# Expert weight matrices fetched in two halves, each with a semaphore of its own

## The chip, the cores and the metric

The kernel runs on one core of a Trainium2 chip. The metric is the device time of one execution in microseconds (us), lower is better. Three runs of the kernel before took 686.67, 686.75 and 687.67 us, a median of 686.75 us.

## What is computed

One Perceiver layer in float32 over 8 batches of 64 tokens with 512 features: a cross attention with a context of 512 rows per batch, a linear attention, and a mixture of 16 experts beside a shared feed-forward network. The change lies in the experts alone. Cut to what matters:

```python
logits = jnp.einsum('bsd,ed->bse', hidden_states, gate_w)
scores = jax.nn.softmax(logits, axis=-1).transpose(0, 2, 1)
topk_w, topk_idx = jax.lax.top_k(scores, cap)              # cap = 8 tokens per batch and expert
x_tok = jnp.take_along_axis(hidden_states[:, None, :, :], topk_idx[..., None], axis=2)
g = jnp.einsum('becd,efd->becf', x_tok, Wg)                # Wg, Wu: 16 x (1024, 512)
u = jnp.einsum('becd,efd->becf', x_tok, Wu)
h = jax.nn.gelu(g, approximate=False) * u
eo = jnp.einsum('becf,edf->becd', h, Wd) * topk_w[..., None]   # Wd: 16 x (512, 1024)
...
shared = jnp.einsum('bsf,df->bsd', jax.nn.gelu(gs, approximate=False) * us, Ws_d)
return out + shared
```

Each expert has three matrices of 2 MB (512 x 1024 floats), so the experts read 48 matrices, 96 MB, from memory.

## The kernel before

The program is written by hand, one instruction stream per engine, tied by semaphores. The attentions come first, then the routing, then from about 421 us the list `ITEMS`: one eighth of the shared network first, then experts 0 and 1, an eighth, experts 2 and 3, an eighth, and so on, ending with expert 15 (`LAST`). A shared eighth is called `("s", i)` and an expert `("e", e)`.

**TensorE (PE).** For item n the order is `item_gate(n)`, `item_transpose(n - 1)`, `item_value(n)`, `item_down(n - 1)`. The first and third are `item_up` (products at L1409): for each of four slices `dt` of the 512 features, the tokens `x_slot` are loaded as weights of the array and `w_g` or `w_u` streams through it, 8 matmul instructions in the program, which the profile shows as 16 records. `item_down` (L1446) does the same with `w_d` and the transposed hidden values `hid_T`, with `j` over four slices. Each group waits once for its matrix, on `wg_in`, `wu_in` or `wd_in`. For the shared eighth the products are L1419 and L1459, with weights that are already on chip.

**The load queue.** The tiles `w_g`, `w_u` and `w_d` are doubled, so matrix e may be fetched when expert e - 2 has used its own. All loads are issued by SyncE (SP) in one fixed order, written out in the `for e in range(2, E, 2)` loop: for each pair of experts g(e), u(e), g(e+1), d(e), u(e+1), d(e+1). Each issue waits until the products of expert e - 2 are done. Transfers of one queue are served in the order of their issue. In memory each matrix lies with its partitions first, so that a partition's 16 KB are one contiguous run. In `w_g` and `w_u` these are the slices `dt` in order; in `w_d` they are the eight slices 0 to 7, of which product `j` reads slices j and 4 + j.

**Results.** The 64 result rows of an expert go by `send_row` (L380), eight transfers of 16 KB from chip memory to chip memory, into `eo_slot`. ScalarE (ACT) issues them for experts 0 to 12 on a queue of its own, SP issues all of expert 13 and the first half of expert 14, behind the last weight loads, and ACT the other half. TensorE sums them at the end (L1564), after a wait for all sends (`eo_sent`), then does `item_transpose(15)` and `item_down(15)`, and the last products (L1571) give the output.

```python
            item_gate(LAST)
            item_value(LAST)

            for par in range(2):
                pe.wait_ge(eo_sent[par], 16 * B * ((E - par) // 2))
```

Of the kernel before, what the change touches and what calls it, by code (L numbers as in the profile page):

```python
# [25 lines left out]
NT = TOK // P  # L26
KT = D // P
# [11 lines left out]
def perceiver_block(nc, x_d, ctx_d, wq_d, bq_d, wk_d, bk_d, wv_d, bv_d, wo_d, bo_d, wqkv_d, proj_d,  # L39
                    wout_d, bout_d, gate_d, wg_d, wu_d, wd_d, wsg_d, wsu_d, wsd_d, out_d):  # L40
    main = ExitStack()
    with main:
# [3 lines left out]
        def sem(name):  # L46
            return main.enter_context(nc.semaphore(name))
# [118 lines left out]
        w_u0 = sb(moe, "w_u0", [P, KT, FF])  # L166
        w_d0 = sb(moe, "w_d0", [P, NF, D])
# [3 lines left out]
        ws_d = sb(moe, "ws_d", [P, NF, D])  # L171
# [47 lines left out]
        w_g0 = sb(moe, "w_g0", [P, KT, FF])  # L219
# [37 lines left out]
        ctx0_in = [sem(f"ctx0_in{dt}") for dt in range(KT)]  # L257
        ctx_in, wqkv_in, wo_in, wout_in, rows_in = (sem(f"{n}_in") for n in ("ctx", "wqkv", "wo", "wout", "rows"))
        proj_in, gate_in = sem("proj_in"), sem("gate_in")
        wg_in, wu_in, wd_in = ([sem(f"{n}_in{i}") for i in range(2)] for n in ("wg", "wu", "wd"))  # L260
        ws_hi_done, ws_split, hid_hi_done, hid_split = sem("ws_hi_done"), sem("ws_split"), sem("hid_hi_done"), sem("hid_split")
        gate_hi_done, gate_split = sem("gate_hi_done"), sem("gate_split")
        wsg_in, wsu_in, wsd_in = sem("wsg_in"), sem("wsu_in"), sem("wsd_in")
# [110 lines left out]
        def g_stripe(i):  # L374

            return (i + 1) % NF

        def send_row(queue, e, b):
            row = SLOTS * (e % 2) + CAP * b
            queue.dma_start(eo_slot[CAP * e:CAP * (e + 1), b, :], eo_of(e)[row:row + CAP, :]).then_inc(eo_sent[e % 2], 16)  # L380
# [13 lines left out]
        @block.sync  # L394
        def _(sp):
            for dt in range(KT):
                sp.dma_start(wk_raw[:, dt], wk_d[:, dt]).then_inc(wk_in[dt], 16)
                sp.dma_start(ctx_raw[:, dt], ctx_d[0, :, dt]).then_inc(ctx0_in[dt], 16)
            for tile, src in ((bias_k, bk_d), (bias_q, bq_d), (bias_v, bv_d)):
                sp.dma_start(tile[:], src).then_inc(bias_in, 16)  # L400
            sp.dma_start(wv_raw[:], wv_d).then_inc(wv_in, 16)
            sp.dma_start(x[:], x_d.rearrange("(t p) d -> p t d", p=P)).then_inc(x_in, 16)
            sp.dma_start(wq_raw[:], wq_d).then_inc(wq_in, 16)
            sp.dma_start(bo_rows[:], bo_d.partition_broadcast(P)).then_inc(rows_in, 16)
            with sp.Fori(1, B) as b:
                sp.wait_ge(ctx_split, b + KT - 1)
                sp.dma_start(ctx_raw[:], ctx_d[b]).then_inc(ctx_in, 16)
            sp.dma_start(w_o[:], wo_d).then_inc(wo_in, 16)
            sp.dma_start(w_qkv[:], wqkv_d).then_inc(wqkv_in, 16)
            sp.wait_ge(x_done, NT)  # L410
            sp.dma_start(bout_rows[:], bout_d.partition_broadcast(P)).then_inc(rows_in, 16)
            for q in range(4):
                sp.dma_start(proj_twice[HD * q:HD * (q + 1)], proj_d[q % 2]).then_inc(proj_in, 16)
            sp.dma_start(w_out[:], wout_d).then_inc(wout_in, 16)
            sp.wait_ge(xbias_done, 2 * NT)
            sp.dma_start(gate[:], gate_d).then_inc(gate_in, 16)
            sp.wait_ge(qkv_lo_dve, KT)
            sp.wait_ge(qkv_lo_pool, 2 * KT)
            sp.dma_start(ws_g[:], wsg_d).then_inc(wsg_in, 16)
            sp.wait_ge(kv_ps, NT * KT)  # L420
            sp.dma_start(ws_u[:], wsu_d).then_inc(wsu_in, 16)
            sp.dma_start(w_u0[:], wu_d[0]).then_inc(wu_in[0], 16)
            sp.dma_start(w_d0[:], wd_d[0]).then_inc(wd_in[0], 16)
            sp.dma_start(ws_d[:], wsd_d).then_inc(wsd_in, 16)
            sp.wait_ge(att_done, 2 * NT)
            sp.dma_start(w_g0[:], wg_d[0]).then_inc(wg_in[0], 16)
            def expert_load(kind, e):

                tiles, src, arrived, used = {"g": (w_g, wg_d, wg_in, g_ps), "u": (w_u, wu_d, wu_in, u_ps),
                                             "d": (w_d, wd_d, wd_in, down_ps)}[kind]  # L430
                if e >= 2:
                    n = AT["e", e - 2]
                    sp.wait_ge(used, downs_upto(n) if kind == "d" else n + 1)
                sp.dma_start(tiles[e % 2][:], src[e]).then_inc(arrived[e % 2], 16)

            expert_load("g", 1)
            expert_load("u", 1)
            for e in range(2, E, 2):
                for kind, ahead in (("g", 0), ("u", 0), ("g", 1)):
                    expert_load(kind, e + ahead)  # L440
                if e == 2:
                    sp.wait_ge(give_ps, 2)
                    sp.wait_ge(last_T_done, NT)
                    expert_load("d", 1)
                for kind, ahead in (("d", 0), ("u", 1), ("d", 1)):
                    expert_load(kind, e + ahead)
            sp.wait_ge(g_ps, AT["s", NF - 2] + 1)
            for e in range(LATE, E - 1):
                sp.wait_ge(eo_done, e + 1)
                for b in range(B if e < E - 2 else B // 2):  # L450
                    send_row(sp, e, b)
            for t in range(NT):
                sp.wait_ge(y_done, t + 1)
                sp.dma_start(out_d[P * t:P * (t + 1), :], x[:, t, :]).then_inc(out_sent, 16)
            sp.wait_ge(out_sent, 16 * NT)
# [670 lines left out]
        def _(pe):  # L1126
# [203 lines left out]
            u = w = a = 0  # L1330
# [67 lines left out]
            def item_up(n, weights, shared_parts, off, in_, done):  # L1398


                dst = 2 * (n % 2) + off
                if n >= 2 and not is_expert(n - 2):
                    pe.wait_ge(sx_done, NT * shared_before(n - 2) + 2)
                if is_expert(n):
                    e = ITEMS[n][1]
                    pe.wait_ge(in_[e % 2], 16 * (e // 2 + 1))
                    for dt in range(KT):
                        for fh in range(2):
                            ins = pe.matmul(ps[64 * fh:64 * (fh + 1), dst, :], x_slot[:, e, dt, :],  # L1409
                                            weights[e % 2][:, dt, BANK * fh:BANK * (fh + 1)],  # L1410
                                            start=(dt == 0), stop=(dt == KT - 1), skip_group_check=True)
                else:
                    i = ITEMS[n][1]
                    hi, lo = shared_parts
                    pe.wait_ge(ws_split, 3 * i + off + 1)
                    for dt in range(KT):
                        w_hi_part, w_lo_part = hi[:, dt, :], lo(i)[:, dt, :]
                        for j, (a, c) in enumerate(((w_hi_part, xn_hi), (w_hi_part, xn_lo_moe), (w_lo_part, xn_hi))):
                            ins = pe.matmul(bank(dst), a, c[:, dt, :], start=(dt == 0 and j == 0),  # L1419
                                            stop=(dt == KT - 1 and j == 2))  # L1420
                ins.then_inc(done, 1)
# [16 lines left out]
            def item_down(n):  # L1438

                if is_expert(n):  # L1440
                    pe.wait_ge(hidT_done, experts_upto(n))
                    e = ITEMS[n][1]
                    pe.wait_ge(wd_in[e % 2], 16 * (e // 2 + 1))
                    for j in range(KT):
                        for fh in range(2):
                            ins = pe.matmul(ps[64 * fh:64 * (fh + 1), 6 + n % 2, :],  # L1446
                                            hid_T[:, n % 2, j, 64 * fh:64 * (fh + 1)], w_d[e % 2][:, KT * fh + j, :],
                                            start=(j == 0), stop=(j == KT - 1), skip_group_check=True)
                    ins.then_inc(down_ps, 1)
                else:  # L1450
                    i = ITEMS[n][1]
                    pe.wait_ge(ws_split, 3 * i + 3)
                    pe.wait_ge(hid_split, shared_before(n) + 1)
                    if shared_before(n):
                        pe.wait_ge(sx_done, NT * shared_before(n))
                    for t in range(NT):
                        rows = slice(P * t, P * (t + 1))
                        for j, (a, c) in enumerate(((hid_hi, ws_d_hi[:]), (hid_lo, ws_d_hi[:]), (hid_hi, ws_d_lo[:, i, :]))):
                            ins = pe.matmul(bank(shared_down_bank(n, t)), a[:, n % 2, rows], c, start=(j == 0), stop=(j == 2))  # L1459
                        ins.then_inc(down_ps, 1)  # L1460
# [46 lines left out]
            for g in range(2 * KT):  # L1507
                dt, pair = g % KT, g // KT
# [112 lines left out]
```

## Time and profile before

| | |
|---|---|
| Median of three runs | 686.75 us |
| The profiled execution's own time | 688.42 us |
| Its span (first to last instruction) | 686.5 us |
| TensorE busy | 647.1 us (94%) |
| VectorE, ScalarE busy | 321.9 us, 252.5 us |
| Mean granted clock of TensorE | 0.987 |
| Bytes moved by DMA | 129.55 MB |

The page divides the span into 40 slices of 17.2 us and gives the busy share of each engine in tenths, the granted clock and the DMA engines' share. For groups of instructions it gives busy time, the mean duration of one and the idle time just before them with what ended it. DMA rows give the median time from the issue of a transfer to its landing. The queue of SP is q1 and that of ACT q10. DMA shares are of 16 DMA engines together.

### The profile page before, as it was taken

To read this page: it belongs to the slowest core of one execution; us is meant where nothing else is said; L and a number is where in the kernel's file an instruction comes from. 1 tells how busy PE (TensorE), PEld (TensorE's weight loads), DVE (VectorE), ACT (ScalarE), POOL (GpSimd) and SP (SyncE) were. 2 spreads that over 40 slices of the span, in tenths; PEclk is the share of its full clock that TensorE was granted. 3 is DMA by queue.
4 is the path that set the end of the run, shared out by engine and by line. 5 is a ranking of instruction groups with operands and counts; after the bars stand their busy time and mean duration, and the time that the engine had idled before them with its cause. 6 is when DMAs were issued, how large, how long until landed. Compare 5 with 4: busy or idle time off the path is not lost.

```text
span 686.5 us, 10386 instructions
## 1 busy us (share of the span) xinstructions
PE 647.1 (94%) x4214; PEld 419.3 (61%) x4214; DVE 321.9 (47%) x653; ACT 252.5 (37%) x482; POOL 31.8 (5%) x33
## 2 busy tenths in 40 slices
PE   6989999999999999799999978999999999998986
PEld 5767777787877776478978455444443544443432
DVE  5964644546263444855778765423223231313122
ACT  4744645445463444355683342111120221121210
POOL 0300000000000000174000000000000000000000
PEclk9999999999999999989999999999999999999999
DMA  8111011010610000213038802799999999999951
GB/s 305 78 62 63 1 63 61 2 62 2 260 48 2 1 1 2 59 50 126 1 137 354 348 21 64 304 402 418 417 413 405 408 405 399 395 382 389 378 200 61
DMA packets 14347, 129.55 MB, mean 189 GB/s; under 512 B 2720, under 2 KB 2848, under 8 KB 6240
## 3 DMA queue, kind: packets, MB, share of 16 engines
q1 hardware_dynamic: 12576, 127.15, 47.0%
q10 hardware_dynamic: 1728, 1.77, 0.8%
q8 instruction: 33, 0.54, 0.3%
q14 instruction: 10, 0.08, 0.0%
HBM read 125.90 MB, written 1.05 MB: 185 GB/s over the span
## 4 chain that ended last, share of the span: by engine, by line
PE 77%; DVE 9%; DMA 7%; ACT 4%; issue 1%; SPq 1%; ACTq 0%; DVEq 0%
PE ps L1141 22%; PE ps L1409 14%; PE ps L1446 8%; PE ps L1324 5%; PE ps L1211 4%; PE ps L1419 4%; DMA w_u<-in_wu 4%; PE ps L1459 3%; PE ps L1288 3%; PE ps L1187 2%; PE ps L1222 2%; PE ps L1252 2%; PE ps L1361 2%; PE ps L1373 1%; DMA w_d<-in_wd 1%
## 5 line engine op out<-in xcount | busy, mean ns | idle before, releaser
L1409 PE MATMUL ps<-w_u,x_slot 128*64 128x512 f32 x256 | 59.5, 607 | 3.0 <-DMA w_u<-in_wu 3.0
L1446 PE MATMUL ps<-w_d,hid_T 128*64 128x512 f32 x256 | 58.2, 596 | 1.8 <-ACT hid_T L710 1.4
L1409 PE MATMUL ps<-w_g,x_slot 128*64 128x512 f32 x256 | 58.1, 595 | 0.8 <-ACT x_slot L729 0.8
L553 ACT ACTIVATE probs<-ps,neg_max 128x512 f32<-128x512 f32 x64 | 43.5, 687 | 39.1 <-DVE neg_max L842 39.1
L822 DVE COPY probs_T<-ps 128x512 f32<-128x512 f32 x32 | 22.1, 691 | 68.7 <-PE ps L1211 68.7
L694 ACT ACTIVATE hid<-ps 128x512 f32<-128x512 f32 x24 | 14.3, 598 | 105.1 <-PE ps L1409 79.5
L1141 PE MATMUL ps<-wv_hi,ctx_hi 128*128 128x512 f32 x128 | 51.6, 403 | 0.1
L1141 PE MATMUL ps<-wv_lo,ctx_hi 128*128 128x512 f32 x128 | 50.0, 391 | 0.0
L1141 PE MATMUL ps<-wv_hi,ctx_lo 128*128 128x512 f32 x128 | 49.9, 390 | 0.0
L1013 DVE TENSOR_TENSOR hid<-hid,ps 128x512 f32<-128x512 f32 x24 | 16.5, 686 | 70.5 <-PE ps L1409 40.8
L842 DVE TENSOR_REDUCE neg_max<-ps 128x1 f32<-128x512 f32 x64 | 39.7, 683 | 18.4 <-PE ps L1187 18.3
L1141 PE MATMUL ps<-ctx_hi,wk_hi 128*128 128x512 f32 x112 | 44.4, 397 | 0.4 <-ACT k_T L538 0.4
L1141 PE MATMUL ps<-ctx_lo,wk_hi 128*128 128x512 f32 x112 | 43.6, 390 | 0.0
L1141 PE MATMUL ps<-ctx_hi,wk_lo 128*128 128x512 f32 x112 | 43.6, 389 | 0.0
L1409 PEld LDWEIGHTS ps<-w_u,x_slot 128*64 128x64 f32 x256 | 18.8, 140 | 37.2 <-issue 37.2
L1446 PEld LDWEIGHTS ps<-w_d,hid_T 128*64 128x64 f32 x256 | 17.8, 137 | 36.2 <-issue 34.3
L538 ACT ACTIVATE k_T<-ps,bias_k 128x512 f32<-128x512 f32 x32 | 21.6, 690 | 48.8 <-PE ps L1141 48.8
L1409 PEld LDWEIGHTS ps<-w_g,x_slot 128*64 128x64 f32 x256 | 18.1, 137 | 35.0 <-issue 34.0
L723 ACT COPY x_slot<-ps 64x512 f32<-64x512 f32 x14 | 8.1, 580 | 82.9 <-PE ps L1446 82.9
L1141 PEld LDWEIGHTS ps<-wv_hi,ctx_hi 128*128 128x128 f32 x128 | 24.0, 188 | 16.5 <-ACT v_s L534 6.2
L835 DVE TENSOR_SCALAR probs<-probs,row_inv 128x512 f32<-128x512 f32 x64 | 31.2, 487 | 2.3
L1211 PE MATMUL ps<-ident,probs 128*128 128x128 f32 x256 | 31.0, 274 | 0.0
(232 smaller groups left out, 1198.8 us busy)
## 6 DMA issues: line engine op xcount, KB each, us to landing
w_u<-in_wu SPq DMA_DIRECT2D x16, 2048.0 KB, 17.9
w_d<-in_wd SPq DMA_DIRECT2D x16, 2048.0 KB, 15.4
w_g<-in_wg SPq DMA_DIRECT2D x16, 2048.0 KB, 15.8
ctx_raw<-in_ctx SPq DMA_DIRECT2D x7, 1024.0 KB, 4.7
w_qkv<-in_wqkv SPq DMA_DIRECT2D x1, 3072.0 KB, 15.3
ws_g<-in_wsg SPq DMA_DIRECT2D x1, 2048.0 KB, 7.9
ws_u<-in_wsu SPq DMA_DIRECT2D x1, 2048.0 KB, 7.9
ws_d<-in_wsd SPq DMA_DIRECT2D x1, 2048.0 KB, 21.2
```

The lines of the kernel that those rows point to most:

```text
L538: act.activation(k_T[:, ht, :], bank(FIRST_K + ht if first else PROJ[ht % 2]), ACT.Identity, bias=bias_k[:, ht:ht + 1], scale=1.0).then_in ...
L553: act.activation(probs[:, p, :], bank(SCORE[p]), ACT.Exp, bias=neg_max[:, p:p + 1], scale=1.0, accum_out=row_sum[:, p:p + 1]).then_inc(exp ...
L822: dve.tensor_copy(probs_T[:, ht % 2, 1].rearrange("p s c -> p (s c)"), bank(TRANS[ht % 2][1])).then_inc(pT_done[1], 1)
L835: dve.tensor_scalar(probs[:, p, :], probs[:, p, :], row_inv[:, p:p + 1], None, ALU.mult).then_inc(prob_done, 1)
L842: dve.tensor_reduce(neg_max[:, p:p + 1], bank(SCORE[p]), AX.X, ALU.max, negate=True).then_inc(max_done, 1)
L1141: ins = pe.matmul(dst, a(dt), c(dt), start=(dt == 0 and i == 0), stop=(dt == KT - 1 and i == 2))
L1211: ins = pe.transpose(ps[:, TRANS[ht % 2][pr], P * st:P * (st + 1)], probs[:, 2 * ht + pr, P * st:P * (st + 1)], ident[:])
L1288: ins = pe.matmul(bank(RES_BANK[k] + t), rows_T[:, dt, P * t:P * (t + 1)], w[:, dt, :], start=(dt == 0), stop=(dt == KT - 1))
L1324: ins = pe.matmul(bank(qkv_bank(n)), a, c, start=(dt == 0 and i == 0), stop=(dt == KT - 1 and i == 2))
L1409: ins = pe.matmul(ps[64 * fh:64 * (fh + 1), dst, :], x_slot[:, e, dt, :], weights[e % 2][:, dt, BANK * fh:BANK * (fh + 1)], start=(dt == 0 ...
L1419: ins = pe.matmul(bank(dst), a, c[:, dt, :], start=(dt == 0 and j == 0), stop=(dt == KT - 1 and j == 2))
L1446: ins = pe.matmul(ps[64 * fh:64 * (fh + 1), 6 + n % 2, :], hid_T[:, n % 2, j, 64 * fh:64 * (fh + 1)], w_d[e % 2][:, KT * fh + j, :], start ...
```

## The change

Every expert matrix is fetched by two transfers of 1 MB in place of one of 2 MB, each with a semaphore of its own, in the same order and behind the same wait for the tile. The first half of `w_g` and `w_u` holds slices `dt` 0 and 1, 8 KB in a run per partition. The first half of `w_d` holds what the products j = 0 and 1 read, slices 0, 1, 4 and 5, and so two runs of 4 KB per partition. TensorE waits for the first half before the first product of a group, and for the second before the fifth.

```diff
-        wg_in, wu_in, wd_in = ([sem(f"{n}_in{i}") for i in range(2)] for n in ("wg", "wu", "wd"))
+        wg_in, wu_in, wd_in = ([[sem(f"{n}_in{i}{half}") for half in "ab"] for i in range(2)] for n in ("wg", "wu", "wd"))
...
+        def half_of(kind, w, half):
+
+            if kind == "d":
+                w = w.rearrange("p (f j) d -> p f j d", f=2)
+                return w[:, :, KT // 2 * half:KT // 2 * (half + 1)]
+            return w[:, KT // 2 * half:KT // 2 * (half + 1)]
...
-            sp.dma_start(w_u0[:], wu_d[0]).then_inc(wu_in[0], 16)
-            sp.dma_start(w_d0[:], wd_d[0]).then_inc(wd_in[0], 16)
-            sp.dma_start(ws_d[:], wsd_d).then_inc(wsd_in, 16)
-            sp.wait_ge(att_done, 2 * NT)
-            sp.dma_start(w_g0[:], wg_d[0]).then_inc(wg_in[0], 16)
             def expert_load(kind, e):
...
-                sp.dma_start(tiles[e % 2][:], src[e]).then_inc(arrived[e % 2], 16)
-
+                for half in range(2):
+                    sp.dma_start(half_of(kind, tiles[e % 2][:], half), half_of(kind, src[e], half)).then_inc(arrived[e % 2][half], 16)
+
+            expert_load("u", 0)
+            expert_load("d", 0)
+            sp.dma_start(ws_d[:], wsd_d).then_inc(wsd_in, 16)
+            sp.wait_ge(att_done, 2 * NT)
+            expert_load("g", 0)
             expert_load("g", 1)
             expert_load("u", 1)
...
-                    pe.wait_ge(in_[e % 2], 16 * (e // 2 + 1))
                     for dt in range(KT):
+                        if dt % (KT // 2) == 0:
+                            pe.wait_ge(in_[e % 2][dt // (KT // 2)], 16 * (e // 2 + 1))
...
-                    pe.wait_ge(wd_in[e % 2], 16 * (e // 2 + 1))
                     for j in range(KT):
+                        if j % (KT // 2) == 0:
+                            pe.wait_ge(wd_in[e % 2][j // (KT // 2)], 16 * (e // 2 + 1))
```

On SP, in the steady part of the load order (experts 4 and 5), there stood before, one row per transfer, with its size in partitions x floats:

```order
L434 DMA w_g<-in_wg 128x4096 [waits g_ps]
L434 DMA w_u<-in_wu 128x4096 [waits u_ps]
L434 DMA w_g<-in_wg 128x4096 [waits g_ps]
L434 DMA w_d<-in_wd 128x4096 [waits down_ps]
L434 DMA w_u<-in_wu 128x4096 [waits u_ps]
L434 DMA w_d<-in_wd 128x4096 [waits down_ps]
```

and now the same stretch reads:

```order
L437 DMA w_g<-in_wg 128x2048 [waits g_ps]
L437 DMA w_g<-in_wg 128x2048
L437 DMA w_u<-in_wu 128x2048 [waits u_ps]
L437 DMA w_u<-in_wu 128x2048
L437 DMA w_g<-in_wg 128x2048 [waits g_ps]
L437 DMA w_g<-in_wg 128x2048
L437 DMA w_d<-in_wd 128x2x1024 [waits down_ps]
L437 DMA w_d<-in_wd 128x2x1024
L437 DMA w_u<-in_wu 128x2048 [waits u_ps]
L437 DMA w_u<-in_wu 128x2048
```

The order of the matrices is unchanged: d(e) still stands before u(e + 1), and each pair of halves is issued behind one wait. A half of `w_d` has two runs of 1024 floats per partition.

On TensorE, around an odd expert, before (w_g, transposes, w_u, then w_d of the expert before):

```order
L1409 MATMUL ps<-w_g,x_slot 64x512 [waits wg_in1,sx_done]
L1409 MATMUL ps<-w_g,x_slot 64x512 x7
L1435 MATMUL ps<-ident,hid 128x128 [waits hid_done]
L1435 MATMUL ps<-ident,hid 128x128 x3
L1409 MATMUL ps<-w_u,x_slot 64x512 [waits wu_in1,sx_done]
L1409 MATMUL ps<-w_u,x_slot 64x512 x7
L1446 MATMUL ps<-w_d,hid_T 64x512 [waits wd_in0,hidT_done]
L1446 MATMUL ps<-w_d,hid_T 64x512 x7
```

and now:

```order
L1418 MATMUL ps<-w_g,x_slot 64x512 [waits wg_in1a,sx_done]
L1418 MATMUL ps<-w_g,x_slot 64x512 x3
L1418 MATMUL ps<-w_g,x_slot 64x512 [waits wg_in1b]
L1418 MATMUL ps<-w_g,x_slot 64x512 x3
L1444 MATMUL ps<-ident,hid 128x128 [waits hid_done]
L1444 MATMUL ps<-ident,hid 128x128 x3
L1418 MATMUL ps<-w_u,x_slot 64x512 [waits wu_in1a,sx_done]
L1418 MATMUL ps<-w_u,x_slot 64x512 x3
L1418 MATMUL ps<-w_u,x_slot 64x512 [waits wu_in1b]
L1418 MATMUL ps<-w_u,x_slot 64x512 x3
L1456 MATMUL ps<-w_d,hid_T 64x512 [waits wd_in0a,hidT_done]
L1456 MATMUL ps<-w_d,hid_T 64x512 x3
```

No product has moved. The fifth of each group of eight carries one more wait, on the second half's semaphore.

## Rows read from the trace of the kernel before

**Rows 1.** The page: DMA engines' share in 40 slices; the group of the w_u products.
```profile
DMA  8111011010610000213038802799999999999951
...
L1409 PE MATMUL ps<-w_u,x_slot 128*64 128x512 f32 x256 | 59.5, 607 | 3.0 <-DMA w_u<-in_wu 3.0
```

**Rows 2.** Windows: PE, PEld, DVE, ACT, POOL busy; then PEclk, DMA share, GB/s.
```profile
460.00:480.00 20.00, 20.00 (x92) 8.75 (x88) 7.30 (x11) 4.32 (x8) 0.00 (x0) 1.00 1.01 421
620.00:640.00 20.00, 16.96 (x74) 7.58 (x72) 5.02 (x8) 3.44 (x7) 0.00 (x0) 0.91 1.00 386
660.00:680.00 20.00, 16.37 (x75) 5.28 (x72) 2.06 (x3) 2.34 (x4) 0.00 (x0) 1.00 0.15 57
```

**Rows 3.** SP's timeline: start us, duration, what is issued.
```profile
445.48 0.81 SPq L434 DMA_DIRECT2D w_d<-in_wd  x2
...
540.12 0.43 SPq L434 DMA_DIRECT2D w_u<-in_wu  x1
...
646.59 0.33 SPq L434 DMA_DIRECT2D w_d<-in_wd  x1
...
662.63 2.62 SPq L380 DMA_DIRECT2D eo_slot<-eo  x4
```

**Rows 4.** DMA view: issue to landing, single transfers issued at 445.48, 540.12 and 646.59.
```profile
w_d<-in_wd SPq DMA_DIRECT2D x1, 2048.0 KB, 7.7
...
w_u<-in_wu SPq DMA_DIRECT2D x1, 2048.0 KB, 19.7
...
w_d<-in_wd SPq DMA_DIRECT2D x1, 2048.0 KB, 20.0
```

**Rows 5.** TensorE's timeline: w_u of expert 9, then the stall at expert 13.
```profile
563.46 3.65 PE L1409 MATMUL ps<-w_u,x_slot 128*64 128x512 f32 x16
...
628.25 5.06 PE L1409 MATMUL ps<-w_u,x_slot 128*64 128x512 f32 x16 [3.04 <-DMA w_u<-in_wu]
633.13 3.62 PE L1446 MATMUL ps<-w_d,hid_T 128*64 128x512 f32 x16
```

**Rows 6.** Chain that ended last, 600 us to the end: start, us, what.
```profile
601.80 26.31 DMA w_u<-in_wu
...
664.82 5.28 DMA eo_slot<-eo
...
670.14 3.65 PE ps L1564 x16
```

**Rows 7.** Windows after the two waits of TensorE, columns as in Rows 2.
```profile
628.00:629.00 1.00, 0.75 (x2) 0.32 (x4) 0.59 (x1) 1.00 (x3) 0.00 (x0) 0.50 1.17 473
...
670.00:674.00 4.00, 3.86 (x19) 1.34 (x20) 0.00 (x0) 0.00 (x0) 0.00 (x0) 1.00 0.00 0
```

**Rows 8.** DMA view, 362 to 375 us: packets, then SP's queue with its share.
```profile
DMA packets 375, 5.39 MB, mean 415 GB/s; under 512 B 46, under 2 KB 46, under 8 KB 46
...
q1 hardware_dynamic: 374, 5.37, 96.5%
```

**Rows 9.** DMA view, landings after issues at 353.63 and 354.10 us.
```profile
w_u<-in_wu SPq DMA_DIRECT2D x1, 2048.0 KB, 12.4
w_d<-in_wd SPq DMA_DIRECT2D x1, 2048.0 KB, 16.8
```

**Rows 10.** DMA view, landings after issues at 6.31, 6.94 and 7.42 us.
```profile
v_s<-in_wv SPq DMA_DIRECT2D x1, 1024.0 KB, 6.9
x<-in_x SPq DMA_DIRECT2D x1, 1024.0 KB, 9.0
o_T<-in_wq SPq DMA_DIRECT2D x1, 1024.0 KB, 11.0
```

**Rows 11.** DMA view, 610 to 625 us: both queues while result rows are sent.
```profile
DMA packets 567, 5.84 MB, mean 389 GB/s; under 512 B 133, under 2 KB 133, under 8 KB 222
...
q10 hardware_dynamic: 182, 0.18, 3.7%
```

## The prediction

> **What bounds the kernel now.** I read the page first, then the windows of the expert stage, then SP's and TensorE's timelines and the chain of waits, and last the DMA view of a few short stretches, to price a transfer.
>
> By the page's group of the `w_u` products TensorE hardly ever waits for a load: 3.0 us in all [rows 1]. That row misleads. The DMA digits beside it are 9 from the 28th slice to the 39th [rows 1], and the windows say it exactly: from 460 us to past 640 the 16 DMA engines are full, a share of 1.01 and 1.00, at 421 GB/s early and 386 GB/s late [rows 2]. Both engines are full at once, and the question is which runs behind the other.
>
> The landings answer it. The load of `w_d` for expert 1 is issued at 445.48 and lands 7.7 us later, the one for expert 15 is issued at 646.59 and takes 20.0 us [rows 3, 4]. So the queue grows: SP issues when a tile comes free, and the transfer waits behind earlier ones. From 453.2 to 666.6 us, 39 transfers land, one in 5.47 us. TensorE's slack shrinks with it. For an odd expert `w_u` stands behind `w_d` of the expert before, though it is used first, and so it is the tightest. For expert 9 it lands at 540.12 + 19.7 = 559.8 and is used at 563.46, a slack of 3.6 us [rows 3 to 5]. For expert 13 it lands 26.31 us after its issue at 601.80, and TensorE has stood still for 3.04 us [rows 5, 6]. The granted clock is then 0.50, which is 1.2 GHz in place of 2.4 [rows 7], and the group takes 633.13 - 628.25 = 4.88 us, where a group at full clock takes some 3.43 (16 records 0.213 us apart; the 3.65 of its row includes the end of the last) [rows 5]. This stall costs 3.04 + 1.45 = 4.5 us.
>
> The end is what matters. The chain of waits goes from expert 14's result to the send of its rows, which takes 5.28 us to land, and only then, at 670.14, TensorE sums [rows 6]. SP's half of these rows was issued at 662.63 on the queue that still held `w_d` of expert 15 until 646.59 + 20.0 = 666.6 [rows 3, 4]. The final sum can't start before the last weights have gone through. From 445 us to there the DMA queue never runs dry, so the end is set by how long 40 loads take, not by when TensorE waits within.
>
> **The change, part by part.**
>
> *Earlier starts.* A group may start when half of its matrix is there, some 2.6 us earlier. Expert 13's `w_u` would then stall 0.4 to 0.7 us for its first half and 0.9 us for its second, in place of 3.04, and the clock would probably stay up: 3 us of TensorE time. At `w_d` of expert 1 a small wait of 0.4 us goes too. I count all of it as nothing, because the load queue covers it. The next issue waits longer for its turn than TensorE gains, and the last load lands when it did. If that cover were gone, these 3 us and more would come off the end.
>
> *The waits and issues.* TensorE gets 48 more waits. Two groups with a wait between them follow each other 3.43 us apart, as 16 records without one would, so a satisfied wait costs under 0.02 us, and that lies under the queue as well. SP issues twice, 0.8 us for two in place of 0.33 [rows 3]. Behind a second issue stands the next wait for a tile, with transfers queued for 13 us and more, so it costs nothing. The sends of SP come after the last load and wait for expert 13's and 14's results anyway.
>
> *The transfers themselves.* This is the term. A packet here is one contiguous run of a partition: 375 - 46 = 329 packets make 5.38 MB, so 16 KB each [rows 8]. They keep the 16 engines busy for 0.965 x 13 us, so one takes 0.61 us. After the change a matrix of gate or value weights is 256 packets of 8 KB in place of 128, and `w_d` is 512 of 4 KB. What a packet costs beyond its bytes I take from landings one behind the other. With 16 KB packets 2 MB land in 370.9 - 366.0 = 4.9 us, 2.45 per MB [rows 9]. With 8 KB packets `o_T` lands at 18.4, 2.5 us after `x`, and with 2 KB packets `x` (four runs of 2 KB per partition) at 15.9, 2.7 us after `v_s` [rows 10]. Per DMA engine a MB is 4, 8 or 32 packets: 28 more packets cost 0.25 us, so 9 ns each, and the middle case fits within the reading of 0.1 us.
>
> In the stretch without a pause there are 40 loads (`w_d` of experts 1 to 15, `w_u` of 3 to 15, `w_g` of 4 to 15). Per DMA engine 25 loads of gate and value weights get 8 more packets each and 15 of `w_d` 24 more, 200 + 360 = 560 packets, 5.0 us. Each second transfer also brings one more semaphore packet per engine, 40 in all, at the same price at most: 0.4 us. **Sum: + 5.4 us** on the landing of the last load. Loads before that stretch have gaps to lose it in.
>
> Bounds. Above: if a run of 4 KB cost as much as one of 2 KB, `w_d` would take 5.4 us in place of 4.9, and gate and value weights by the landing of `o_T` 5.0, which makes 15 x 0.5 + 25 x 0.1 = 10. Below: nothing, if a packet's overhead is hidden while sixteen engines compete anyway. They are not at their best now (5.47 us per load against 4.9), so even a gain can't be excluded, see the rivals. I take 5.4, from the nearest rows.
>
> *The end.* With + 5.4 the last load lands at 672.0. TensorE itself would arrive about 2.5 us late. Going through the groups with landings shifted by this sum, its first and second halves wait 0.9 and 0.9 us at `w_u` 11, 3.3 and 0.9 at `w_u` 13, 0.5 and 0.9 at `w_d` 14, 7.4 us in all, against 4.5 + 0.4 saved. It would then stand some 5 us before the final sum, not 2.07. After 3.04 us the clock fell, after the 2.07 us at 670 it did not [rows 7]. That could add 0 to 1.45 us; most of a low stretch would pass while TensorE stands, so I take 0.
>
> **Forecast: 686.75 + 5.4 = 692.1 us.** The profiled execution has 688.42 and a span of 686.5; against these it is 693.8 and 691.9. The runs shown are 1.7 us faster than the profiled one, so their queue may be a little less behind, but a span of 684.8 is still 3 us over 686.5 - 4.5 - 0.4 = 681.6, what TensorE would need without its stalls for loads. From here on, 0.2% (1.4 us) is about what a measurement can tell from no change.
>
> **The rivals.**
>
> *A packet costs less* (0.13). The landings are read to 0.1 us, so 28 packets may cost 0.1 in place of 0.25 us, near 3.5 ns each, and 560 packets 2.0 us. With semaphores 2 to 2.4: 689.0. The Trainium skill ("DMA: Bandwidth & Descriptors", section "Why small descriptors are slow (HBM only)") says this: some 3 cycles of overhead per packet beside one cycle per 32 bytes. By that rule a 16 KB packet is 515 cycles, two of 8 KB 518 and four of 4 KB 524, so gate and value weights would take 0.03 us longer and `w_d` 0.09, 2.0 us in all and 688.8. The rows speak for two to three times that.
>
> *A dearer half of w_d* (0.13). Two runs with a gap in memory, or a pause between transfers. Price up to the bound above with the slow clock at the end: + 8 to 11, 695 to 698. Against it: 97% share in a stretch of full queue [rows 8] leaves little room for pauses.
>
> *Nothing* (0.13). The overhead is hidden, the last load lands at 666.6 as before, and the final sum starts at 670: 686.75, within 1.4.
>
> *Faster* (0.15). The engines' loss grows when ACT's queue is busy: 389 GB/s with a share of 3.7% for the sends, against 415 with none [rows 8, 11]. Loads lose 40 x 0.57 = 22 us so, far more than the 2 KB rows themselves need. If this comes from 2 KB rows standing behind 16 KB packets, smaller packets mend part of it. From a quarter (5.4 of 22) on, the last load lands no later than before, and beyond that the half waits pay: expert 14's result comes 2.6 us earlier, and so does the send. That gives 684.1, and 681.9 if all stalls go. For it: only the sends' share differs between these windows. Against it: a row may as well disturb by its bytes and by its ports, which the change leaves.
>
> **How the numbers follow.** The likeliest case has 0.46 with a range of its own of 690.5 to 694.5. It, the cheap packet and the dear half are slower by more than 0.2%: 0.46 + 0.13 + 0.13 = 0.72. Nothing: 0.13. Faster: 0.15. The range leaves out the lower half of the faster case and the upper half of the dear one, and so reaches from 684.5 to 696.
>
> **What would show it.** Right: the DMA packets of the page rise by some 11,000 to 25,400; the landing of the last `w_d` moves to about 672; GB/s in the windows from 460 us fall by 2% (421 to about 412); stalls of TensorE for `w_u` 11 and 13 are split in two; the wait before the final sum grows from 2.07 to some 5 us. Wrong: the last load lands at 667 or before, or the sends land early although it lands late, or windows with sends move more than 389 GB/s.

## The result and the profile after

The changed kernel takes 699.63 us (six runs, 698.25 to 701.2) against 687.1 us for the kernel before beside it (six runs, 686.3 to 689.23). The ratio is 1.0175, 95% interval 1.0157 to 1.0193: 12.5 us slower. The forecast was 692.1 with a range to 696. The direction and the place were right, the size was not: it came out at more than twice the 5.4 us.

The profiled execution took 700.16 us with a span of 698.4 us. From its page: the busy engines, the granted clock and the DMA share by slice, the packets, and the three groups of expert products.

```profile
PE 652.5 (93%) x4214; PEld 419.1 (60%) x4214; DVE 321.8 (46%) x653; ACT 252.7 (36%) x482; POOL 32.2 (5%) x33
...
PEclk9999999999999999899999999999999999899998
DMA  8111011010700000303077606799999999999941
...
DMA packets 25356, 129.57 MB, mean 186 GB/s; under 512 B 3488, under 2 KB 3616, under 8 KB 15200
...
L1418 PE MATMUL ps<-w_u,x_slot 128*64 128x512 f32 x256 | 60.9, 615 | 7.8 <-DMA w_u<-in_wu 7.6
L1456 PE MATMUL ps<-w_d,hid_T 128*64 128x512 f32 x256 | 58.9, 600 | 2.6 <-DMA w_d<-in_wd 1.9
L1418 PE MATMUL ps<-w_g,x_slot 128*64 128x512 f32 x256 | 58.1, 595 | 0.8 <-ACT x_slot L737 0.8
```

The same bytes now travel in 11,000 more packets, as forecast. TensorE waits 7.6 us for `w_u`, not less than the 3.0 of [rows 1] but more, though each wait is for half a matrix.

The windows over two long stretches show the queue. The columns are those of [rows 2]. Before:

```profile
470.00:520.00 50.00, 50.00 (x230) 23.28 (x230) 13.31 (x20) 10.84 (x20) 0.00 (x0) 1.00 1.01 416
600.00:650.00 50.00, 46.96 (x210) 22.20 (x208) 11.37 (x17) 8.73 (x16) 0.00 (x0) 0.97 1.01 385
```

and after:

```profile
470.00:520.00 50.00, 50.00 (x230) 22.99 (x228) 13.35 (x20) 10.16 (x19) 0.00 (x0) 1.00 1.02 403
600.00:650.00 50.00, 46.69 (x202) 21.59 (x202) 11.37 (x17) 8.15 (x15) 0.00 (x0) 0.94 1.02 373
```

The DMA engines are as full as before and move 3% less in both. I had forecast 2%.

The last load: SP's timeline of the changed kernel, and then the landings of the two halves of `w_d` of expert 15, to hold against [rows 3, 4].

```profile
652.18 6.22 SPq L437 DMA_DIRECT2D w_d<-in_wd  x2
658.50 7.04 SPq L387 DMA_DIRECT2D eo_slot<-x_slot  x8
669.60 2.62 SPq L387 DMA_DIRECT2D eo_slot<-eo  x4
```

```profile
DMA to landing us min/median/max: 21.5/22.7/23.8
```

The second half is issued at about 652.8 and lands 23.8 us later, at 676.6 in place of 666.6: 10.0 us late. TensorE's timeline shows what follows, at `w_u` of experts 11 and 13, at `w_d` of expert 14 and at the final sum:

```profile
597.97 2.45 PE L1418 MATMUL ps<-w_u,x_slot 128*64 128x512 f32 x8 [2.65 <-DMA w_u<-in_wu]
601.83 3.68 PE L1418 MATMUL ps<-w_u,x_slot 128*64 128x512 f32 x8 [1.42 <-DMA w_u<-in_wu]
...
633.21 1.94 PE L1418 MATMUL ps<-w_u,x_slot 128*64 128x512 f32 x8
636.96 1.94 PE L1418 MATMUL ps<-w_u,x_slot 128*64 128x512 f32 x8 [1.81 <-DMA w_u<-in_wu]
...
663.79 1.94 PE L1456 MATMUL ps<-w_d,hid_T 128*64 128x512 f32 x8 [1.39 <-DMA w_d<-in_wd]
...
679.57 6.13 PE L1574 MATMUL ps<-eo_slot,give 120*64 120x512 f32 x16 [4.53 <-DMA eo_slot<-eo]
```

A group of 16 records now stands as two of 8 with a wait between them. The final sum starts at 679.57 in place of 670.14 [rows 6], 9.4 us late, after a wait of 4.5 us in place of 2.07. It then takes 6.13 us where it took 3.65, since the clock has fallen: a window of the changed kernel, PEclk 0.50, which is 1.2 GHz.

```profile
679.00:681.00 2.00, 1.43 (x4) 0.53 (x6) 0.00 (x0) 0.00 (x0) 0.00 (x0) 0.50 0.00 0
```

The span grew by 9.4 + 2.5 = 11.9 us, 698.4 against 686.5. In the profiled execution that is the whole change, and all of it is made of the late last load and the slow clock behind it.

### The profile page after: what moved, and what is told of

It reads as the page before. It is cut to its first block, busy times and chain, and to the rows that moved or that the text cites. A ratio compares the mean times of both kernels' runs of the same rounds, so it can differ in the third digit from the quotient of the medians.

```text
span 698.4 us, 10434 instructions
## 1 busy us (share of the span) xinstructions
PE 652.5 (93%) x4214; PEld 419.1 (60%) x4214; DVE 321.8 (46%) x653; ACT 252.7 (36%) x482; POOL 32.2 (5%) x33
## 4 chain that ended last, share of the span: by engine, by line
PE 66%; DMA 17%; DVE 9%; ACT 4%; SPq 2%; issue 1%; ACTq 0%; DVEq 0%
PE ps L1149 22%; DMA w_u<-in_wu 11%; PE ps L1418 9%; PE ps L1456 6%; PE ps L1332 4%; PE ps L1219 4%; DMA w_d<-in_wd 3%; PE ps L1296 3%; PE ps L1428 2%; PE ps L1195 2%; PE ps L1230 2%; PE ps L1469 2%; PE ps L1260 2%; PE ps L1369 2%; PE ps L1381 1%
## 5 line engine op out<-in xcount | busy, mean ns | idle before, releaser
L1418 PE MATMUL ps<-w_u,x_slot 128*64 128x512 f32 x256 | 60.9, 615 | 7.8 <-DMA w_u<-in_wu 7.6
```

## The experiments

Two questions were open: whether packets or transfers are what costs, and why the queue lost 10 us where the price of the packets gave 5.4. In what follows "last load" is the landing of `w_d` of expert 15 in the one profiled execution. Four kernels with whole matrices (the kernel before and three further down) gave 664.5 to 668.5 us for it, three with all halves 673.6 to 679.2, so one value is good to 2 or 3 us. The means of these groups, 666.4 and 676.5, are 10 us apart as well. Times are medians; ratios are to the kernel before on the same chip, with their 95% interval.

### Packets or transfers

**Only gate and value matrices in halves.** `w_d` is one transfer with one wait again.

```diff
+                if kind == "d":
+                    sp.dma_start(tiles[e % 2][:], src[e]).then_inc(arrived[e % 2][0], 16)
+                else:
+                    for half in range(2):
...
```

> Gate and value matrices in halves, w_d whole: 25 of the 40 further transfers and 200 of the 560 further packets per DMA engine. Packet theory (loss goes with the number of packets): the last load of w_d lands 10.0 x 200/560 = 3.6 us later than before, time +3.5 to +5. Transfer theory (each further transfer costs the same, whatever its packets): 10.0 x 25/40 = 6.3 us later, time +6 to +9.

Measured 692.33 us, ratio 1.0075 (1.0042 to 1.0108). The last load lands at 670.7, 4.1 us late.

**Only w_d in halves.**

```diff
+                if kind != "d":
+                    sp.dma_start(tiles[e % 2][:], src[e]).then_inc(arrived[e % 2][0], 16)
+                else:
+                    for half in range(2):
...
```

> Only w_d in halves of two 4 KB runs: 15 of 40 transfers, 360 of 560 packets. Packet theory: last load +6.4 us, time +6.5 to +9. Transfer theory: +3.7 us, time +3.5 to +5.

Measured 695.92 us, ratio 1.0123 (1.0089 to 1.0156). Last load 672.2, 5.6 us late.

**All in halves, w_d with runs of 8 KB.** Its eight slices are stored in the order 0, 4, 1, 5, 2, 6, 3, 7.

```diff
-                w = w.rearrange("p (f j) d -> p f j d", f=2)
-                return w[:, :, KT // 2 * half:KT // 2 * (half + 1)]
+                return w[:, KT * half:KT * (half + 1)]
...
-                                            hid_T[:, n % 2, j, 64 * fh:64 * (fh + 1)], w_d[e % 2][:, KT * fh + j, :],
+                                            hid_T[:, n % 2, j, 64 * fh:64 * (fh + 1)], w_d[e % 2][:, 2 * j + fh, :],
```

> All matrices in halves as in the change, but w_d laid out in memory and on chip so that a half is one run of 8 KB per partition: all 40 further transfers, 320 packets in place of 560. Packet theory: last load +5.7 us, time +6 to +8. Transfer theory: +10.0 us, time +12.5.

Measured 693.94 us, ratio 1.0116 (1.0073 to 1.016). Last load 670.8, 4.3 us late.

**Whole matrices, w_d in runs of 4 KB.** The kernel before, with a gap of 4 KB behind each 4 KB of `w_d` in memory.

```diff
-                sp.dma_start(tiles[e % 2][:], src[e]).then_inc(arrived[e % 2], 16)
+                if kind == "d":
+                    sp.dma_start(tiles[e % 2][:].rearrange("p (r j) d -> p r (j d)", j=2), src[e, :, :, 0]).then_inc(arrived[e % 2], 16)
...
```

> The kernel before, but w_d lies in memory in runs of 4 KB with gaps: one transfer, one semaphore and one wait as before, 360 further packets and no further transfer. Packet theory: last load +6.4 us, time +6.5 to +9. Transfer theory: no change.

Measured 693.78 us, ratio 1.0103 (1.0066 to 1.014). Last load 671.2, 4.6 us late. Its page, and the final sum in its timeline:

```profile
span 691.0 us, 10386 instructions
...
DMA packets 20491, 129.55 MB, mean 187 GB/s; under 512 B 2720, under 2 KB 2848, under 8 KB 14432
```

```profile
674.71 3.65 PE L1567 MATMUL ps<-eo_slot,give 120*64 120x512 f32 x16 [3.27 <-DMA eo_slot<-eo]
```

This run decides between the two. Nothing has changed but the length of the runs and the gaps between them in memory: 48 transfers as before, one semaphore each, one wait each. It is 1% slower, where the transfer theory says no change. The third run says the same from the other side: with all the transfers but 8 KB runs, the last load is 4.3 us late in place of 10.0. And the first two add up, 4.1 + 5.6 = 9.7 against 10.0 for both. The loss goes with the number of packets. It is not in strict proportion: the four kernels lost 4.1, 5.6, 4.3 and 4.6 us for 200, 360, 320 and 360 further packets, where the packet theory said 3.6, 6.4, 5.7 and 6.4. What the gaps in memory do by themselves was not tested; the halves of gate and value matrices are single runs of 8 KB and cost their 4.1 us without such gaps inside a half. A small part for the transfers themselves can't be excluded: with the same packets, 15 more transfers read 695.92 against 693.78, intervals overlapping.

### What the packets meet

In the two next kernels ACT sends no result row while weights are loaded. All rows of experts 0 to 12 follow the last load, so only the landings can be compared, not the time.

```diff
-                if 1 < n < LAST:
-                    send(n)
...
             act.wait_ge(eo_done, E - 1)
+            for par in range(2):
+                act.wait_ge(wd_in[par], 16 * (E // 2))
+            for e in range(LATE):
+                for b in STRIPES:
+                    send_row(act, e, b)
```

> The kernel before, but ACT issues no result row while weights are loaded: all rows of experts 0 to 12 go at the end, behind the last load (some 70 us longer for their issue). To be read in the landings alone. If the sends stretch the loads: a load of 16 KB packets takes 4.9 us each time, the queue no longer grows, w_d of expert 15 lands within 10 us of its issue, TensorE has no stall for a load, and the windows from 460 us show a DMA share below 1. If the loads compete with something else: 5.5 us per load and a growing queue as before.

> The changed kernel with the same edit. If the further loss over the price of a packet (+ 4 to 5 us) comes from sends and packets together, it goes with the sends: halves land 2.49 us (8 KB packets) and 2.54 us (4 KB) apart, the queue does not grow, and the last load lands within 1 us of the one of the run before. If small packets are dearer by themselves under a full queue, halves land 2.7 us or more apart without sends too.

They took 752.18 and 749.77 us (one run each). The windows of the kernel before without sends:

```profile
470.00:520.00 50.00, 50.00 (x231) 23.10 (x231) 13.35 (x20) 10.55 (x20) 0.00 (x0) 1.00 1.01 425
600.00:650.00 50.00, 50.00 (x228) 23.82 (x225) 13.59 (x21) 9.83 (x18) 0.00 (x0) 1.00 0.97 398
```

and of the changed kernel without sends:

```profile
470.00:520.00 50.00, 50.00 (x230) 23.04 (x228) 12.06 (x18) 9.73 (x18) 0.00 (x0) 1.00 1.02 416
600.00:650.00 50.00, 49.33 (x228) 23.54 (x228) 14.31 (x22) 9.31 (x17) 0.00 (x0) 1.00 1.00 399
```

Early both queues are full and move 425 and 416 GB/s, the bare price of small packets, 2%. Later the DMA engines of the kernel before have time to spare, and those of the changed one stay full. The windows from 540 to 560 us, first before, then changed:

```profile
540.00:560.00 20.00, 20.00 (x93) 10.02 (x93) 6.35 (x10) 2.86 (x6) 0.00 (x0) 1.00 0.98 398
540.00:560.00 20.00, 20.00 (x91) 8.79 (x91) 5.45 (x8) 2.52 (x6) 0.00 (x0) 1.00 1.02 415
```

TensorE never waits for `w_u` in either. The last load lands at 641.34 + 10.2 = 651.5 in the one and at 651.1 in the other, 15 and 25 us earlier than with sends. The changed kernel ran ahead of the other here, with the last `w_d` issued at 638.92 against 641.34, so up to 2 us may be hidden in this comparison. **Without sends the halves cost the last load 2 us at most**, as most of their 5 us fit into the time that the DMA engines have to spare. With sends they have none.

These two kernels also give the bare price from the landings. The median time between neighbouring ones is 4.90 us for a whole matrix, 2.49 us for a half in 8 KB packets and 2.55 us for a half in 4 KB packets. So a gate or value matrix in halves costs 0.09 us more and `w_d` 0.21, and 25 x 0.09 + 15 x 0.21 = 5.4 us, the term of the prediction. The other 4.6 of the 10.0 us appear only with the sends.

The traces of the two kernels with sends tell how much dearer a send has become. I fitted the time between neighbouring landings, from 453 us on, by a constant and a price per row packet of ACT's queue (some 857 in each kernel). Before: 4.93 us per matrix and 24.4 ns per packet. After: 2.53 us per half, 5.07 per matrix, and 29.1 ns. By this fit the constant gives 39.5 x 0.136 = 5.4 us and the sends 857 x 4.7 ns = 4.0 us more. Another 0.7 us stands ahead of the stretch (`w_d` of expert 1 lands at 453.9, not 453.2). That these add up to 10.1 is no proof, since such a fit always returns the length of its stretch. Nor is one pair of fits: the standard errors of the two constants make 4 us over all loads, and those of the prices are 3.4 and 1.8 ns. What shows the difference is that it repeats. Four kernels with whole matrices in 16 KB packets give 23.2 to 25.7 ns per row packet. Five with smaller packets give 28.4 to 31.7 ns, among them all halves at 8 KB with 28.4 and whole matrices with `w_d` at 4 KB with 29.0.

**The sends on the queue of the loads.** The kernel before; SP issues the rows of experts 0 to 12, behind each pair's loads, in place of ACT.

```diff
                 for kind, ahead in (("d", 0), ("u", 1), ("d", 1)):
                     expert_load(kind, e + ahead)
+                sp_sends(AT["e", e - 1])
```

> The kernel before, with the rows of experts 0 to 12 issued by SP on the queue of the loads in place of ACT on its own. Same bytes, same rows. If the stretch comes from DMA engines that serve two queues in turn, it goes: the last load lands up to 15 us earlier (limited by TensorE to some 6), time -3 to -5. If it comes from the rows' own bytes and the on-chip memory they read and write, the last load lands as before or a few us later, time 0 to +5.

Measured 694.26 us, ratio 1.0093 (1.0061 to 1.0125), the last load at 665.9. SP's timeline tells why this says little:

```profile
580.94 0.33 SPq L434 DMA_DIRECT2D w_d<-in_wd  x1
581.31 12.73 SPq L380 DMA_DIRECT2D eo_slot<-x_slot  x19
594.09 0.44 SPq L434 DMA_DIRECT2D w_g<-in_wg  x1
```

Issuing 19 sends takes SP 12.7 us, in which no load is issued. Most loads with no send between them landed 4.9 us apart, but the blocks of sends and the late issues took back what that won. Whether a send costs by its bytes or by the second queue stays open.

### What the halves are worth to TensorE

**Both waits ahead.** The changed kernel, but TensorE waits for both halves before the first product of a group.

```diff
+                    for half in range(2):
+                        pe.wait_ge(in_[e % 2][half], 16 * (e // 2 + 1))
                     for dt in range(KT):
-                        if dt % (KT // 2) == 0:
-                            pe.wait_ge(in_[e % 2][dt // (KT // 2)], 16 * (e // 2 + 1))
...
```

> The changed kernel, but TensorE waits for both halves ahead of the first product: all of the cost and none of the earlier starts. If the load queue sets the end, as predicted, the last load lands as in the changed kernel and the time is its 699.6 within 1.5 (a little more, 0 to 2, where a longer stall brings the slow clock). If the earlier starts are worth their 2.6 us each at the stalls, it is 3 to 8 us slower than the changed kernel.

Measured 696.93 us, ratio 1.0151 (1.0121 to 1.018). That overlaps with the 1.0175 (1.0157 to 1.0193) of the changed kernel and is on the fast side, below the 698 to 701 us expected. The early starts bring no gain that can be seen. Its last load landed at 673.6, and I can't say whether the 3 us between the two are more than scatter.

### Where the end is set

**Order alone.** The kernel before with `w_u` of the odd expert ahead of `w_d` of the even one, and in the last pair `w_d` of 14 ahead of `w_g` of 15.

```diff
-                for kind, ahead in (("g", 0), ("u", 0), ("g", 1)):
+                for kind, ahead in (("g", 0), ("u", 0), ("g", 1))[:3 if e < E - 2 else 2]:
...
-                for kind, ahead in (("d", 0), ("u", 1), ("d", 1)):
+                for kind, ahead in (("u", 1), ("d", 0), ("d", 1)) if e < E - 2 else (("d", 0), ("g", 1), ("u", 1), ("d", 1)):
```

> The kernel before with whole matrices, the load order alone changed: w_u of the odd expert ahead of w_d of the even one, and for the last pair w_d of expert 14 ahead of w_g of expert 15. If the queue sets the end: TensorE's stall at w_u of expert 13 (3.0 us and 1.45 us of slow clock) goes, the last load still lands within 1.5 us of 666.6, SP's rows behind it land at 670, and the time is 687 within 1.5. If TensorE's own path sets it: 4 to 5 us faster, 682.5.

Measured 689.08 us, ratio 1.0018 (0.9998 to 1.0037): no change. The stall at `w_u` of 13 is gone, and this is where it went, in TensorE's timeline:

```profile
667.56 6.59 PE L1564 MATMUL ps<-eo_slot,give 120*64 120x512 f32 x16 [4.72 <-DMA eo_slot<-eo]
```

TensorE arrives earlier and waits 4.7 us for the rows behind the last load (which landed at 664.5), then runs at the slow clock, as in the changed kernel. The sum starts 2.6 us earlier than before and takes 2.9 us longer, so that the slow clock alone takes back what the earlier landing gave in this execution.

**The last rows on GpSimd's queue.** The kernel before; GpSimd sends the rows of expert 13 and the first half of 14, with a semaphore of its own.

```diff
-            for e in range(LATE, E - 1):
-                sp.wait_ge(eo_done, e + 1)
-                for b in range(B if e < E - 2 else B // 2):
-                    send_row(sp, e, b)
...
+            pool.wait_ge(g_ps, AT["s", NF - 2] + 1)
+            for e in range(LATE, E - 1):
+                pool.wait_ge(eo_done, e + 1)
...
```

> The kernel before, the rows that SP sends behind the last load (expert 13 and half of 14) issued by GpSimd on a queue of its own. The final sum no longer waits for the last load but for expert 14's result (w_d of 14, second last but one in the queue) and 3 to 6 us for its sends: theory of the queue: 0 to 2 us earlier, 685 to 687, since expert 14's result comes no earlier in this order.

Measured 687.59 us, ratio 1.0005 (0.9984 to 1.0025): no change.

**Both together.**

> Both edits together: w_d of 14 lands some 5.5 us earlier, its result some 4 us earlier with the stall at 13 gone, and its rows don't stand behind the last load. Theory of the queue: final sum at 665 to 667 in place of 670, time 683 to 684.5, more than either edit alone. If the sends of GpSimd are slow to issue or land: 687 or more.

Measured 686.0 us, ratio 0.9985 (0.9969 to 1.0001), with a span of 683.0 in the profiled execution. There the final sum starts 3.5 us earlier than before:

```profile
666.64 3.65 PE L1567 MATMUL ps<-eo_slot,give 120*64 120x512 f32 x16 [2.33 <-DMA eo_slot<-eo]
```

The final sum starts at the time expected, 665 to 667, but the time is not the 683 to 684.5 I had named. `w_u` of 15 now lands only at 660.5, and TensorE waits 1.4 us for it. The 1.3 us between the medians can't be told from no change, so neither edit alone nor both together show a gain. This kernel has the lowest median of the study, no more.

**The halves on top of it.**

> The changed kernel with the order and the GpSimd rows of the run before. If halves cost through the load queue wherever its end is read, w_d of 14 and the last load land 9 to 10 us later than in that run (658 and 675 to 676), and the time is 7 to 10 us over its 686.0. If only the wait behind the last load made the halves dear, it is within 2 us of it.

Measured 695.14 us, ratio 1.0105 (1.0061 to 1.0149). `w_d` of 14 landed at 663.3 in place of 648.6 and the last load at 679.2 in place of 666.1, 3 to 5 us later than expected. Against the kernel without halves, 0.9985 on its ratio, the halves cost about 8 us here too, though no row of SP stands behind the last load any more. The cost is the queue's, not the tail's.

## Why the prediction was right and wrong

*What bounds the kernel: right.* The load queue sets the end. Removing TensorE's stall by order alone changed nothing, and removing the sends moved the last load by 15 us. One reading was off by one: the 9s of the DMA digits stand in the 27th to the 38th slice, not the 28th to the 39th. Nothing hangs on it.

*Earlier starts, counted as nothing: right.* With both waits ahead the kernel is no slower. The stalls were split as described, but not spread as forecast. They began at `w_u` of expert 9, where the second half waits 1.74 us and I had forecast none. At 11 they were longer, 2.65 and 1.42 us in place of 0.9 and 0.9, and at 13 shorter, 1.81 in place of 3.3 and 0.9.

*The price of a packet: right.* 5.4 us by 9 ns each; the landings without sends give 5.4, and the kernels with 200 to 560 more packets line up by packets, not by transfers. The rival "a packet costs less", with 3.5 ns, falls. By the Trainium skill ("DMA: Bandwidth & Descriptors", section "Why small descriptors are slow (HBM only)"), with some 3 cycles per packet, the estimate was 2.0 us. The measurement differs, and it decides.

*The sum on the landing of the last load, + 5.4: this is the step that failed.* It measured + 10.0. I took what the queue loses to the sends, 22 us before, as a constant, and asked only whether smaller packets might mend it (the rival "faster"). They made it worse: a row packet of ACT costs the loads 29.1 in place of 24.4 ns, some 4 us over all. Why it does is not shown. The term was missing from the sum, and the upper bound of 10 us, built from a dearer packet alone, held it only by luck.

*The slow clock at the end, taken as 0 between 0 and 1.45: wrong.* The final sum lost 2.5 us, with most of it at 1.2 GHz. I had argued that most of the low stretch would pass while TensorE stands. The one comparable row was a stall of 3.04 us with a loss of 1.45, and with a wait of some 5 us in the forecast, nothing in the rows spoke for a loss of 0. The length of a wait does not give the loss either, see the last section, so that a term from 0 to 3 us was what could be said.

*The rivals.* "A dearer half of `w_d`" came nearest in size (695 to 698, still under the 699.63 measured), but not in cause, since gate and value halves cost their share too. The range ended at 696 because I gave that case only its lower half. "Nothing" came near, within 2 us on the last load, in the kernel without sends.

## What to carry to other kernels

When transfers run back to back for two hundred us, cutting them finer is paid in every packet and returned only where the receiver stands still, and if the queue sets the end, not even there. Before changing the size of a packet, look at what else uses the DMA engines in that stretch: the loss to the other stream is not a constant. And a stall that is removed has to be followed to the next thing that waits for the queue, here the rows behind the last load.

## What the runs showed of the hardware

An issue takes longer when many transfers have not landed. Before, each issue of a load on SP took 0.33 to 0.43 us, with at most four loads outstanding. In the changed kernel the last two halves of `w_d` took 6.22 us to issue together, the second with eight halves outstanding, at most 88 weight packets for each DMA engine. Its other issues of 1.5 us and more, from 555 us on and up to 4.4 us, all have eight or nine halves outstanding. That the queue could not take more is my reading of it. I see no harm from it here, as each of these transfers was still far from its turn.

A send of eight rows of 2 KB carries 16 KB but delays a full stream of loads by 8 x 24.4 ns = 0.20 us before the change, where 16 KB of load take 0.04 us (4.9 us for 2 MB). By that fit some 107 sends cost 21 us of queue time before the change and 25 after it.

Before the final sum TensorE stood for 2.07 us and kept its clock; it stood for 4.5 and 4.7 us and ran the group of 16 in 6.13 and 6.59 us in place of 3.65. Between these there is no simple order. The kernel with `w_d` in runs of 4 KB stood for 3.27 us and lost nothing, the one with `w_d` in halves stood for 3.15 and took 5.35, and the one with the sends on SP stood for 7.19 and took 5.75.
